# A MoE block on one core: a new opening for attention, and a last sequence that leaves in two halves

## The reference

```python
# layer 0: attention with 16 heads over one shared key/value head, then a mixture of experts
xn = layernorm(x, g_in); q = xn @ Wq; k, v = split(xn @ Wkv)         # a null key and value go first
sim = q @ k.T + bias; causal; keys whose mask is False get -max      # softmax, @ v, @ Wo, layernorm(g_out)
x = x + sum_e [expert(token) == e] * (relu(h @ W1[e] + b1[e]) @ W2[e] + b2[e])   # top 1 of 8, with capacity
# layer 1: top 2 of 8 gated experts per token and a shared one give z; then, per sequence:
logits = z.mean(axis=tokens) @ gate_w.T + gate_b                     # 8 logits per sequence, the top 2 kept
out = x + sum_{two best e} gate[e] * gelu(z @ expert_w[e].T + expert_b[e])
```

## Time and profile before

| | |
|---|---|
| median of 3 runs | 588.13 us |
| the profiled execution | 587.29 us |
| its span, first to last instruction | 585.6 us |
| granted TensorE clock, mean | 0.997 |
| PE busy in the span | 552.7 us (94%) |
| DVE, ACT, POOL busy | 317.1, 242.2, 233.2 us |

### The profile page before, as it was taken

How to read it: one execution, slowest core, us unless ns; L and a number is a source line. 1 busy time by engine, 2 the same in 40 slices (tenths; PEclk the granted TensorE clock), 3 DMA queues, 4 the chain that set the end, 5 groups by cost and what they waited for, 6 DMA issues and landing times.

```text
span 585.6 us, 11470 instructions
## 1 busy us (share of the span) xinstructions
PE 552.7 (94%) x3806; PEld 462.3 (79%) x3806; DVE 317.1 (54%) x965; ACT 242.2 (41%) x669; POOL 233.2 (40%) x319
## 2 busy tenths in 40 slices
PE   3899999988999999999999999999999998998885
PEld 3788887744999999988888978888888886775664
DVE  2777767676222335743447754444444445765664
ACT  1465545660211111115544245555555454443432
POOL 1412211041111121006645375555555078787860
PEclk9999999999999999999999999999999999999998
DMA  5980000185995532513397036656665233655552
GB/s 131 338 365 2 2 1 2 63 364 241 304 351 187 181 112 73 155 55 73 82 278 228 1 83 163 160 159 159 159 162 159 82 90 117 189 173 169 165 178 75
DMA packets 53208, 88.31 MB, mean 151 GB/s; under 512 B 11251, under 2 KB 43892, under 8 KB 51605
## 3 DMA queue, kind: packets, MB, share of 16 engines
q1 hardware_dynamic: 45028, 65.29, 32.4%
q0 software_dynamic: 8112, 22.16, 16.0%
HBM read 62.38 MB, written 25.04 MB: 149 GB/s over the span
## 4 chain that ended last, share of the span: by engine, by line
PE 69%; POOL 13%; DVE 6%; issue 5%; SPq 2%; DMA 2%; ACT 1%; POOLq 0%; ACTq 0%; DVEq 0%
POOL arena L918 11%; PE psum L1564 10%; PE psum L1315 10%; PE psum L1328 9%; PE psum L1476 7%; PE psum L1578 6%; PE psum L1171 5%; PE psum L1143 4%; PE psum L1493 3%; PE psum L1556 3%; POOL iota_i L948 2%; PE psum L1151 1%; PE psum L1511 1%; PE psum L1572 1%; PE psum L1165 1%
## 5 line engine op out<-in xcount | busy, mean ns | idle before, releaser
L918 POOL DMA_INDIRECT arena<-x,row_tok x71 | 68.2, 960 | 52.0 <-PE psum L1556 43.6
L918 POOL DMA_INDIRECT arena<-y_sorted,pos_k_i x64 | 65.2, 1019 | 34.9 <-POOL iota_i L948 18.9
L1564 PE MATMUL psum<-big_w,arena 128*128 x284 | 72.9, 379 | 0.0
L1639 PE MATMUL psum<-big_w,arena 128*128 x256 | 62.9, 379 | 0.0
L1877 ACT ACTIVATE arena<-psum,arena 128x128 f32<-128x128 f32 x64 | 18.2, 368 | 106.6 <-PE psum L1315 84.6
L1315 PEld LDWEIGHTS psum<-arena,big_w 128*128 128x128 f32 x512 | 59.5, 192 | 1.7 <-issue 1.0
L1315 PE MATMUL psum<-arena,big_w 128*128 128x128 f32 x512 | 59.8, 275 | 0.8 <-DVE arena L2565 0.8
L1476 PE MATMUL psum<-arena,big_w 128*128 128x256 f32 x256 | 59.9, 381 | 0.2 <-ACT arena L1896 0.2
L1564 PEld LDWEIGHTS psum<-big_w,arena 128*128 128x128 f32 x284 | 53.8, 190 | 7.1
L1328 PE MATMUL psum<-arena 128*128 128x256 f32 (+1 forms) x256 | 57.7, 380 | 0.0
L1476 PEld LDWEIGHTS psum<-arena,big_w 128*128 128x128 f32 x256 | 47.4, 191 | 7.0 <-ACT arena L1896 0.9
(11 more groups left out here) (327 smaller groups left out, 984.7 us busy)
## 6 DMA issues: line engine op xcount, KB each, us to landing
y_sorted<-arena SPq DMA_DIRECT2D x71, 128.0 KB, 2.6
big_w<-w SPq DMA_DIRECT2D x8, 1024.0 KB, 5.8
tokens<-x SPq DMA_DIRECT2D x4, 1024.0 KB, 14.6
x<-tokens SPq DMA_DIRECT2D x16, 256.0 KB, 2.6
z_kept<-arena SPq DMA_DIRECT2D x16, 256.0 KB, 3.4
out<-arena SPq DMA_DIRECT2D x16, 256.0 KB, 2.6
y_late<-arena SPq DMA_DIRECT2D x16, 128.0 KB, 1.8
big_w<-expert_w_t SPq DMA_DIRECT2D x1, 2048.0 KB, 8.6
```

What stands on the lines that cost most here:

```text
L918: pool.indirect_dma_start(dst, None, rows, bass.IndirectOffsetOnAxis(ap=idx, axis=0)).then_inc(done, 16)
L1564: mm = pe.matmul(bank[2 + i % RT][:, 0:2 * M1], c_gt[i % RT][:, k, :], mgu_s[:, k, bass.ds(e, 1), :].rearrange("p a m -> p (a m)"), start= ...
L1639: mm = pe.matmul(o, z_t[u][:, k, n * P:(n + 1) * P], ew_s[:, k, bass.ds(e, 1), :].rearrange("p a d -> p (a d)"), start=False, stop=n == NB ...
```

## The change

Opening: the broadcast of the mask by DMA goes. DVE copies the late mask (already in one partition) to bf16, PE multiplies it with a column of ones into two PSUM banks (two products 128x512), and DVE makes `pen_l` from PSUM. `v_null` counts with the null loads, so POOL waits for the four bias loads alone. POOL adds the penalty first and copies the null bias after. PE issues 2 idle products before it reads the flag and 5 after; the late way is now the `If` with `attend_late(0)` to `(2)` in it, then comes the general way as `Else`, and a second `If(late)` holds `attend_late(3)` to `(7)` and what follows.

Tail: in step 15 PE does bias and first half of the second expert of sequence 14 ahead of `turn_z(15)`, the other half behind `gate_logits(15)`. The second expert of sequence 15 (`last_choice`) uses two PSUM banks, 128 tokens in each with a bias product of its own, and gelu, weighing and store go in two halves. The four gathers of sequence 15 count on three semaphores, and DVE's sum waits for them one by one.

```diff
 # SP
-                sp.dma_start(pen_u8.rearrange("p (b k) -> p b k", b=B),
-                             mask.rearrange("a (b s) -> (a b) s", s=S)[:, KEY0:S].partition_broadcast(P)).then_inc(l_pen, 16)
-                sp.dma_start(v_null, null_kv[1:2, :].rearrange("a d -> (a d)").partition_broadcast(P)).then_inc(ld_bias, 16)
+                sp.dma_start(v_null, null_kv[1:2, :].rearrange("a d -> (a d)").partition_broadcast(P)).then_inc(ld_w, 16)
...
             for b in range(B + 2):
-                if b >= 2:
+                if 2 <= b <= B:
                     sp.wait_ge(d_res, b - 1)
                     sp.dma_start(outr[:, (b - 2) * NB:(b - 1) * NB, :], res[(b - 2) % RT]).then_inc(d_st[(b - 2) % RT], 16)
...
+            sp.wait_ge(half_res, TILES2 + 1)
+            sp.dma_start(outr[:, (B - 1) * NB, :], res[(B - 1) % RT][:, 0, :]).then_inc(half_st, 16)
+            sp.wait_ge(d_res, B)
+            sp.dma_start(outr[:, (B - 1) * NB + 1, :], res[(B - 1) % RT][:, 1, :]).then_inc(d_st[(B - 1) % RT], 16)
+            sp.wait_ge(half_st, half_st0 + 16)
 # POOL
-                pool.wait_ge(ld_bias, 80)
+                pool.wait_ge(ld_bias, 64)
...
+                pool.wait_ge(gconst, 2)
+                pool.wait_ge(gsetup, 1)
+                masked_bias(0, slots)
+                pool.wait_ge(slots, 2)
+                pool.wait_ge(gsetup, 3)
+                for t in range(2):
+                    pool.tensor_copy(bias_p[t][:, :, null_at[t]], bias_l[:, :, QL]).then_inc(l_bp, 1)
...
+                parts = ([(n, k, d_got[b % RT]) for n in range(NB) for k in range(2)] if b < B - 1 else
+                         [(0, 0, last_got[0]), (1, 0, last_got[0]), (0, 1, last_got[1]), (1, 1, d_got[b % RT])])
 # PE
+            NEAR = 3
             pe.wait_ge(const, NCONST)
-            general = branch(pe)
-            with pe.If(general):
+            idle_products(2)
+            late = early_keys(pe) == 0
+            with pe.If(late):
+                idle_products(5)
+                turn_late_x(0)
+                pe.wait_ge(l_pen, 1)
+                half = B * QL // 2
+                for u in range(2):
+                    mm = pe.matmul(bank[4 + u][:, 0:half], ones_bf[0:1, :], pen_row[0:1, u * half:(u + 1) * half], start=True, stop=True)
+                mm.then_inc(l_pen, 1)
+                pe.wait_ge(ld_kv, 32)
+                pe.wait_ge(setup, 1)
+                project_late_kv(0)
+                pe.wait_ge(ld_q, 16)
+                project_late_q(0)
+                for c in range(NEAR):
+                    attend_late(c)
+            with pe.Else():
...
-            with pe.Else():
-                turn_late_x(0)
...
-                for c in range(NTW):
+            with pe.If(late):
+                for c in range(NEAR, NTW):
                     attend_late(c)
...
+                ahead = b == B - 1
+                if ahead:
+                    gated_bias(b - 1, 1, ids[b - 1][1])
+                    gated(b - 1, v, 1, 0, ids[b - 1][1])
                 if front:
                     turn_z(b, u)
...
+            def last_choice(b, u, e):
+                pe.wait_ge(d_ge, 2 * b)
+                for n in range(NB):
+                    o = bank[(3, 5)[n]][:, 0:D]
+                    pe.matmul(o, ones_bf[:, :], eb_rows[:, bass.ds(e * D, D)], start=True, stop=False)
+                    for k in range(KD):
+                        mm = pe.matmul(o, z_t[u][:, k, n * P:(n + 1) * P], ew_s[:, k, bass.ds(e, 1), :].rearrange("p a d -> p (a d)"),
+                                       start=False, stop=k == KD - 1)
+                    mm.then_inc((half_e, d_e)[n], 1)
 # ACT
+            def last_gelu():
+                act.wait_ge(d_res, B - 1)
+                act.wait_ge(half_e, TILES2 + 1)
+                act.activation(ge[1][:, 0, :], bank[3][:, 0:D], ACT.Gelu).then_inc(half_ge, 1)
+                act.wait_ge(d_e, 2 * B)
+                act.activation(ge[1][:, 1, :], bank[5][:, 0:D], ACT.Gelu).then_inc(d_ge, 1)
 # DVE
+                dve.tensor_copy(pen_row.rearrange("p (b k) -> p b k", b=B), mv[:, :, KEY0:S]).then_inc(l_pen, 1)
...
+                dve.wait_ge(l_pen, 2)
+                dve.tensor_scalar(pen_l.rearrange("p (u b) k -> p u (b k)", u=2), psum[:, 4:6, 0:B * QL // 2],
+                                  BIG, -BIG, ALU.mult, ALU.add).then_inc(gsetup, 1)
+                dve.wait_ge(ld_w, 16 * (NLDN + 1))
...
-            next(outs[B - 1], None)
+            u = (B - 1) % RT
+            dve.wait_ge(d_r1, B)
+            dve.wait_ge(half_ge, TILES2 + 1)
+            dve.scalar_tensor_tensor(res[u][:, 0, :], ge[1][:, 0, :], gsort[u][:, 1:2], res[u][:, 0, :], ALU.mult, ALU.add).then_inc(half_res, 1)
+            dve.wait_ge(d_ge, 2 * B)
+            dve.scalar_tensor_tensor(res[u][:, 1, :], ge[1][:, 1, :], gsort[u][:, 1:2], res[u][:, 1, :], ALU.mult, ALU.add).then_inc(d_res, 1)
```

More of the change, by code:

```diff
@@ L167, in bass_adaln_ffn_kernel @@
         ht_l = tokens[:, 0:NTW + 1, :]
-        pen_u8 = L.take(B * QL // 4).bitcast(U8)
+        pen_row = L.take(B * QL // 2, rows=1).bitcast(BF16)
         pen_l = L.take(B, QL)
@@ L565, in bass_adaln_ffn_kernel @@
         l_over, l_over0 = x_ev, NTW
+        half_e, half_ge, half_res, half_st = c_mt, c_lk, c_md, c_st[0]
+        half_st0 = 16 * len(range(0, TILES2, RT))
+        last_got = c_got[0:2]
+        last_got0 = [16 * len(range(u, TILES2, RT)) for u in range(2)]
         l_rows_ev, l_beat_g, ld_rest = ld_x[2], ld_x[1], ld_x[3]
@@ L886, in _, with masked_bias @@
                                        pattern=[[0, NPAIR], [-1, QL]], channel_multiplier=1).then_inc(gconst, 1)
-                pool.wait_ge(gconst, 2)
-                pool.wait_ge(gsetup, 2)
-                for t in range(2):
-                    pool.tensor_copy(bias_p[t][:, :, null_at[t]], bias_l[:, :, QL]).then_inc(slots, 1)
-                pool.wait_ge(slots, 2)
-                pool.wait_ge(gsetup, 5)
-                def masked_bias(c, first):
+                def masked_bias(c, done):
                     for t in range(2):
-                        if not first:
+                        if done is l_bp:
                             hold(pool, l_sub, 2 * c - 1 + t)
                         pool.tensor_tensor(bias_p[t][:, :, keys_at[t]], bias_l[:, :, 0:QL],
-                                           pen_l[:, bass.ds(2 * c + t, 1), :].broadcast_to([P, NPAIR, QL]), ALU.add).then_inc(l_bp, 1)
-                masked_bias(0, True)
+                                           pen_l[:, bass.ds(2 * c + t, 1), :].broadcast_to([P, NPAIR, QL]), ALU.add).then_inc(done, 1)
+                pool.wait_ge(gconst, 2)
[5 more added lines that the diff above has]
+                    pool.tensor_copy(bias_p[t][:, :, null_at[t]], bias_l[:, :, QL]).then_inc(l_bp, 1)
                 pool.iota(token_i[:, 0:NTW], [[P, NTW]], base=1, channel_multiplier=1).then_inc(slots, 1)
@@ L994, in _ @@
                     pool.wait_ge(d_z, b - RT + 1)
-                for n in range(NB):
-                    for k in range(2):
-                        gather_rows(yk[b % RT][:, 2 * n + k, :], y2_dram, pos_k_i[:, b * NB + n, k:k + 1], d_got[b % RT])
-                        space()
+                parts = ([(n, k, d_got[b % RT]) for n in range(NB) for k in range(2)] if b < B - 1 else
+                         [(0, 0, last_got[0]), (1, 0, last_got[0]), (0, 1, last_got[1]), (1, 1, d_got[b % RT])])
+                for n, k, done in parts:
+                    gather_rows(yk[b % RT][:, 2 * n + k, :], y2_dram, pos_k_i[:, b * NB + n, k:k + 1], done)
+                    space()
         @block.tensor
@@ L1114, in attend, with idle_products_in @@
                 project_o(b)
+            def idle_products_in(bk, n):
+                for _ in range(n):
+                    pe.matmul(bk.rearrange("p (a b) -> p a b", a=4), ones_bf[:, :],
+                              ones_bf[:, :].unsqueeze(1).broadcast_to([P, 4, P]), start=True, stop=True)
             def idle_products(n):
-                for _ in range(n):
-                    pe.matmul(bank[7].rearrange("p (a b) -> p a b", a=4), ones_bf[:, :],
-                              ones_bf[:, :].unsqueeze(1).broadcast_to([P, 4, P]), start=True, stop=True)
+                idle_products_in(bank[7], n)
             def turn_late_x(c):
@@ L1663, in gated_step @@
                     gate_logits(b)
-                if back:
+                if back and not front:
+                    last_choice(b - 1, v, ids[b - 1][1])
+                elif back and not ahead:
                     gated_bias(b - 1, 1, ids[b - 1][1])
-                    for n in range(NB):
-                        gated(b - 1, v, 1, n, ids[b - 1][1])
+                    gated(b - 1, v, 1, 0, ids[b - 1][1])
+                if back and front:
+                    gated(b - 1, v, 1, 1, ids[b - 1][1])
                 if front:
                     first_expert(b, u)
+            def last_choice(b, u, e):
```

(9 more changed lines are left out.)

19 lines of the change are left out of this document (6 added, 13 removed).

## The result

| | before | after |
|---|---|---|
| median (range, runs) | 588.61 us (587.03 to 592.13, 20) | 587.52 us (584.12 to 589.19, 20) |
| ratio, with its 95% interval | | 0.9968 [0.9954, 0.9983] |
| the profiled execution, its span | 587.29, 585.6 us | 587.56, 585.8 us |

The ratio, which compares runs of both kernels beside each other, says 1.9 us faster (1.0 to 2.7) of 588.6. The forecast was 586.3 of 588.13, 1.85 us. The quotient of the two medians, 0.9981, lies in the same interval, near its end. The two profiled spans don't show the gain: the execution profiled of before lies 1.3 us under its kernel's median, that of after on its own. So the spans as a whole can't be compared; their parts can.

What follows compares the result with a forecast made beforehand. Bounds: the opening's chain to DVE's first add, PE in attention, PE's products then gelu, weighing and store in the tail. −2.9 + 0.95 + 0.1 = −1.85 from 588.13 gives 586.3 us, range 585.2 to 588.5.

Steps and rivals of the forecast that it cites:

- the opening: Start to DVE's first bias add: at 16.75 instead of 19.64 us, 2.9 us earlier, bounds 1.5 and 3.4.
- the jump: PE's branch over the general way between attention turns 2 and 3: +0.95 us, 0.9 exposed, bounds 0.7 and 1.8.
- The stall and POOL's way: Opening: `v_null`'s 3.49 us issue stall goes with the broadcast; POOL's triangle, penalty and null copy done at 16.3 to 17.0.
- Ahead of their users: Opening: null loads come 3.5 us or so earlier, at about 13 us, before anything needs them.
- PE's way: Opening: PE's queries and scores let DVE add at 15.7 us at best, 18.1 at worst.
- I take 16.5 for a level that rises in the middle: Opening: PE's clock reaches 2.4 GHz midway through the query products, so DVE can add at 16.5 us.
- a first add after 18: Opening: sign that the prediction is wrong, DVE's first bias add later than 18 us.
- the clock rival: Opening: PE's clock stays low through the queries; add at 18.1, −1.5 for −2.9, total 587.7 us; chance 0.14.
- the sequencer runs ahead: Attention turn 3: PE's sequencer leads the array by 2.75 us, which hides part of the jump.
- The rival of a jump felt in full: End of turn 2: 3.5 to 4.3 us all exposed, total 588.8 to 589.6 us; chance 0.16.
- The tail: Last sequences: later `turn_z(15)` and second bias against halved gelu, weighing and store; sum +0.1 us, bounds −0.6 and +0.6.
- The store: Tail: the last store has half its bytes, 0.3 us less, bounds 0 and 1.0.

Runs made afterwards that it cites:

- e12: The changed kernel (after) once more, unchanged; 586.78 us, ratio 0.9967.
- e11: After with the mask's DMA broadcast to all 128 partitions put back ahead of `v_null`; 588.12 us, one run (before 588.16).
- e1: Before with the new opening alone, including the near branch and the jump behind turn 2; 588.26 us, ratio 1.0005.
- e3: After with PE's code for the general mask left out, so the branch has nothing to jump over; 586.51 us, ratio 0.9975.
- e5: After with PE's jump moved ahead of the turning of the probabilities of turn 2; 585.9 us, ratio 0.9942.
- e9: After with PE's old order in step 15, no early products of sequence 14, halves kept; 586.52 us, ratio 0.9970.
- e7: After with e5's jump, e9's tail and more idle products in the opening; 584.99 us, ratio 0.9933.
- e4: After with PE's general way in front again, one jump at the start, 13 idle products queued ahead of it; 585.28 us, ratio 0.9952.
- e6: e4 with three idle products behind the penalty products and three behind the first keys; 585.7 us, ratio 0.9945.
- e10: e7 with DVE's null key copy ahead of its null bias copies, PE waiting for it alone; 582.74 us, ratio 0.9908.
- e2: Before with the new tail alone; 587.41 us, ratio 0.9992.
- e8: After with the mask's broadcast put back ahead of `v_null`, to 127 partitions; 602.3 us, one run (before 589.39 on that chip).

## Why the prediction was right, and where not

**The time.** −1.85 forecast, −1.9 measured (−2.7 to −1.0; e12 has −1.9 again). That it came out so closely is partly luck. What the traces show by parts is −2.0 for the opening (a mean, below), +0.8 for the jump and nothing for tail and store (end − sum 15.90 to 16.11, mean 15.99, in the five traces of this tail with a last jump of 4.0 to 4.3 us, against 15.93 and 15.98 with the old tail): −1.2. That is inside the interval, near its end. The other 0.7 us was found in no part; a shorter last jump, as e12 has it (−0.7 at the span's end), could supply it, but the runs without a trace don't show theirs.

**The stall and POOL's way: right in size.** The stall goes with the broadcast (e11 brings it back), `side` lands at 12.0, and triangle, penalty and null copies are through at 16.5, in 16.3 to 17.0. The mask row's copy and `pen_l` cost nothing, hidden as said, the latter 1.23 us instead of 1.4. What the sum left out are DVE's copies of null bias and null key. "Ahead of their users" held only just: beside POOL's adds the bias copies took 1.51 us, and POOL waited 0.18 us for them.

**PE's way: the step that was too large.** "I take 16.5 for a level that rises in the middle" fails: the array worked from 4.6 on, from 4.4 to 10.6 it was busy for 5.86 of 6.20 us, and the level rose only at 15.4, with PE's way at 18.2, beyond its worst bound of 18.1. The prediction had named "a first add after 18" as a sign of being wrong, and both traces of the changed kernel (18.20, and 18.14 in e12) show that sign. The traces with this opening (after, e1, e3, e5, e9, e12) have the rise anywhere from 12.4 to 15.4 and the add from 16.82 to 18.20, with a mean of 17.63. So the term is −2.0, not −2.9; in the profiled run of after it is −1.44, which is the clock rival's case. The rival was right on the place and, in three of six traces, on the size. A high level alone would not have given 15.7 either: in e5, with the level high from 12.4, and in e7, with all queries at 275 ns, PE's scores wait for the null key until 16.06 and 16.41. DVE's copies were at nothing in the sum of PE's way. Before, the add stands at 19.64 or 19.74, held by POOL, and the clock is at no price: with POOL's waits gone the clock, and behind it the null key, became the bound. e4 shows why products early on don't suffice. In e6, e7 and e10, with more of them up to the queries, all queries run at 275 ns, though small gaps stayed (0.53 us before the queries of e10).

**The jump: right.** +0.95 forecast, +0.81 measured, from 3.312 us less a lead of 2.5 where I had 3.46 + 0.2 less 2.75 ("the sequencer runs ahead"). A first `If` that falls through costs 92 ns. The rival of a jump felt in full is out. The Trainium skill, "Runtime: NRT & Kernel Launch", Instruction fetch mechanics, has a taken branch outside the loaded window wait for a fetch of the target's page; the runs agree, with 3.29 to 3.81 us over the general way and 0.07 when nothing lies between. The 108 ns of the Trainium skill, "Advanced Engine Details and Errata", Control Flow Timing, come near the second alone.

**The tail: right in sum, by terms that were off both ways.** `turn_z(15)` is late by 0.86, as forecast (0.87). From there PE does better than I had it: the choice is read faster, and the bias comes at 576.00, 0.31 after that of before instead of 0.62; the second bias costs nothing for the 0.22 forecast, since two products of half the width are one whole one (e9). The last product ends 0.47 later than before. Gelu gives −0.22 and the last weighing −0.27, forecast −0.23 and −0.32. Together 11.34 us from the sum to the last weighing's end, against 11.37: nothing, where I had +0.4. "DVE's tie chain and `weigh(14)` end before the last gelu" is true and misses the point: `weigh(14)` ends at 579.31, before the last gelu at 580.10, but the gelu of the first half waits 0.60 us for it, and DVE then still has the first expert of sequence 15 (to 579.98) and the weighing of the first half, and comes free at 580.5, just as the last gelu ends. From the later choice on, this DVE chain is the bound, and it eats what the halves give. The store: −0.3 forecast. From the last weighing's end to the span's end it is 4.56 before, 4.77 in after and 3.86 in e12, so two traces of one kernel differ by 0.9. The issue of the last store isn't the reason: it takes 1.59 us in after, 0.62 in e12, but 0.38 in before and 0.72 in e3, which end late as well. What goes with it is the price of the last jump, as told at the table. PE reaches that jump 9.7 us behind the sum in after and e12 and 8.9 behind it in before and e9, since the number that it reads comes from DVE's search for ties. So the late choice is felt there once more. The forecast had no such term.

**What stays open.** The stretch of 64 choices (from 341 us to the last ACT copy of that line) has the same instructions in all kernels and lasted 123.2 us in the profile of before, 124.8 in after, 124.1 in e10 and 126.6 in e3. The last copies, before, then e3:

```profile
L1960 ACT COPY arena<-psum x71: 372/372/373, 348.5 to 464.2; 128x256 f32<-128x256 f32 x71
```

```profile
L1964 ACT COPY arena<-psum x71: 372/372/373, 345.4 to 465.1; 128x256 f32<-128x256 f32 x71
```

e3 enters it 2.5 us ahead and leaves it 1.0 behind. PE's busy time in it is 122.2 us before and 123.6 in e3, so most of what is added is idling. I take it for the run and not the kernel, since neither opening nor tail sets it apart (126.2 in e1, 125.7 in e2), but no experiment was made on it. It is why e3, 2.6 us ahead at the 273 mark, ends with a span no shorter than that of before, and why single spans say little here. In four traces (e5, e7, e9, e11) the granted clock also falls to half for 3.4 to 6.8 us around 540 us; before and after have none of that.

## What to carry to other kernels

Removing a stall hands the path to the next thing that is late: list what that is and what it depends on, small copies on a shared engine too, and if it is TensorE's level, keep the array busy right up to the work that counts, not only early. A far jump costs 3.3 to 4.3 us of the sequencer and not of the array: put it where the engine's queue is long or the next instruction waits for another engine anyway. Before an instruction is put in front of others to fill a gap, see whether the gap, in the order that it displaces, was not shorter than the work (0.22 us against 1.09 here).

## Not expected of the hardware

- The array busy from 4.6 us on didn't bring the level of 2.4 GHz before 15.4 in one trace and 12.4 in another of the same opening; and in e4 the level was lost again behind a stretch of 3.3 us in which the array was busy for 2.52, the next stretch at a granted 0.51.
- A broadcast to 127 partitions made the issue behind it take 15.64 us, with 9 GB/s on all DMA engines; one to 128 partitions 2.52 (3.49 in the earlier trace rows, with 158 GB/s).
- Two DVE copies of 64x8 took 0.37 us with POOL idle (before, e2, e8) and 1.25 to 2.01 beside POOL's 128x512 adds (nine traces).
- The last of two stores of 128 KB took 0.62 to 1.59 us to issue half a microsecond behind the other, and 0.33 or 0.34 when 0.84 apart; why it varies was not tried.
- The same taken branch took 3.30 us in one trace of a kernel and 4.26 in another (e12, after).
